# Layer 1 of a two-layer gated cross-attention kernel: the queries' rounding, the block transposition and the output's low part change places

## The reference, cut to what matters

```
q = rms_norm(latents @ Wq);  k = rms_norm(concat(context, latents) @ Wk);  v = concat(...) @ Wv
scores = einsum('bhgqd,bhkd->bhgqk', qg, k) / sqrt(128)
probs  = softmax(scores)
out    = einsum('bhgqk,bhkd->bhgqd', probs, v)
x      = x + tanh(g_xattn[1]) * (out @ Wo)
```

## Time and profile before

| | before |
|---|---|
| median of three runs | 1704.34 us |
| the profiled execution | 1706.54 us, its span 1704.7 us |
| PE busy | 1643.4 us (96%) |
| DVE busy | 1230.3 us (72%) |
| ACT busy | 1022.6 us (60%) |
| POOL busy | 589.8 us (35%) |
| first and last `nb` of layer 1's units | 958.4 and 1663.7 us |

### The profile page before, as it was taken

The page is one execution under the profiler, slowest core; times in us unless marked ns, Lnnn a source line. Parts: engine busy times, 40 slices in busy tenths (PEclk is TensorE's granted clock), DMA queues, the critical chain, the costliest instruction groups (busy, mean ns, idle before and its releaser), DMA issues.

```text
span 1704.7 us, 30549 instructions
## 1 busy us (share of the span) xinstructions
PE 1643.4 (96%) x9757; PEld 1436.2 (84%) x9757; DVE 1230.3 (72%) x2274; ACT 1022.6 (60%) x2511; POOL 589.8 (35%) x584
## 2 busy tenths in 40 slices
PE   9999999999999999999999799999999999999987
PEld 8899999999988888888888678888888888888875
DVE  6444437676787777877778677878787878777775
ACT  5344443345867677677766566666666666666652
POOL 3422223211334444444335333333333333333332
PEclk9999999999999999999999899999999999999999
DMA  6444444535233333333332243434343434343322
GB/s 231 171 166 148 148 171 157 191 133 182 72 106 102 120 98 111 113 95 126 98 106 82 72 136 122 148 119 146 118 159 123 145 123 148 123 148 111 115 93 97
DMA packets 126671, 220.43 MB, mean 129 GB/s; under 512 B 11664, under 2 KB 96016, under 8 KB 123024
## 3 DMA queue, kind: packets, MB, share of 16 engines
q1 hardware_dynamic: 126608, 219.63, 38.6%
HBM read 141.99 MB, written 77.59 MB: 129 GB/s over the span
## 4 chain that ended last, share of the span: by engine, by line
PE 58%; DVE 20%; ACT 9%; DMA 6%; issue 5%; SPq 1%; POOL 1%; DVEq 0%; ACTq 0%; POOLq 0%
PE bank L2134 20%; PE bank L2079 8%; PE bank L2080 8%; PE bank L2081 8%; PE bank L2311 6%; ACT p L1235 4%; DMA probabilities_transposed<-blocks_of_probabilities 2%; DMA blocks_of_probabilities<-probabilities_in_blocks 2%; DVE pt_lo L1957 2%; PE bank L2269 2%; PE bank L2347 2%; DVE probabilities_in_blocks L1966 2%; PE bank L2431 2%; DVE w_lo L1896 2%; DVE wl L1575 1%
## 5 line engine op out<-in xcount | busy, mean ns | idle before, releaser
L630 POOL TENSOR_TENSOR q_r<-q_ms,half 128x4 f32<-128x4 f32 x64 | 64.4, 1007 | 378.5 <-DVE q_ms L1922 378.5
L2079 PE MATMUL bank<-w_hi,xt_hi 128*128 (+2 forms) x512 | 173.4, 339 | 0.1
L2080 PE MATMUL bank<-w_lo,xt_hi 128*128 (+2 forms) x512 | 173.2, 338 | 0.0
L2081 PE MATMUL bank<-w_hi,xt_lo 128*128 (+2 forms) x512 | 172.0, 336 | 0.0
L711 POOL TENSOR_TENSOR pr<-pr,rn 128x512 f32<-128x512 f32 x64 | 67.5, 1055 | 291.4 <-DVE rn L1600 291.4
L1235 ACT ACTIVATE p<-bank,nb,q_r 128x256 f32<-128x256 f32 x256 | 141.4, 576 | 7.4 <-DVE nb L1943 7.4
L764 POOL TENSOR_TENSOR p<-p,rn 128x512 f32<-128x512 f32 x128 | 133.1, 1041 | 28.7 <-DVE rn L1948 25.2
L1244 ACT ACTIVATE pt_hi<-probabilities_transposed 128x1024 fp32r<-128x1024 f32 x64 | 68.0, 1063 | 94.6 <-DMA probabilities_transposed<-blocks_of_probabilities 94.6
L1075 ACT ACTIVATE pr<-sc,nmax 128x128 f32<-128x128 f32 x256 | 99.9, 391 | 40.0 <-DVE nmax L1585 39.6
L2079 PE MATMUL bank<-w_hi,ot_hi 128*128 (+1 forms) x256 | 107.3, 419 | 16.7 <-DVE ot_lo L1971 15.8
L2079 PE MATMUL bank<-w0o_hi,ot_hi 128*128 128x512 f32 x256 | 105.4, 412 | 5.0 <-DVE residual L1592 4.5
(11 more groups left out here) (292 smaller groups left out, 5574.6 us busy)
## 6 DMA issues: line engine op xcount, KB each, us to landing
blocks_of_probabilities<-probabilities_in_blocks SPq DMA_DIRECT2D x64, 512.0 KB, 2.7
probabilities_transposed<-blocks_of_probabilities SPq DMA_DIRECT2D x256, 128.0 KB, 2.8
stage<-w SPq DMA_DIRECT2D x35, 512.0 KB, 3.3
keys_of_layer<-kout SPq DMA_DIRECT2D x16, 1024.0 KB, 4.8
values_of_layer<-vout SPq DMA_DIRECT2D x16, 1024.0 KB, 5.2
kt<-keys_of_layer SPq DMA_DIRECT2D x64, 256.0 KB, 3.3
vs<-values_of_layer SPq DMA_DIRECT2D x64, 256.0 KB, 2.8
vraw<-wv SPq DMA_DIRECT2D x10, 1024.0 KB, 6.7
```

The lines of the kernel that those rows point to most:

```text
L630: pool.tensor_tensor(dst, src, exponent, ALU.pow).then_inc(done, 1)
L2079: nc.tensor.matmul(out_ap, l_hi, r_hi, start=(c == 0), stop=False)
L2080: nc.tensor.matmul(out_ap, l_hi, r_lo, start=False, stop=False)
L2081: op = nc.tensor.matmul(out_ap, l_lo, r_hi, start=False, stop=(c == n - 1))
```

## The change

On ACT, the roundings `qt_hi` and `kt_hi` of unit i+1 go ahead of the four exponentials of unit i. On DVE, `qt_lo` and `kt_lo` go ahead of the reciprocals; the two reciprocals are parted, with `v_low` between them; the block transposition of unit i goes ahead of `probabilities_lo` of i-1; `split_lo` goes from before the accumulation to after `probabilities_lo`; and `output1_lo` goes ahead of `maxima1`. No instruction is added or removed, and PE, POOL and SP keep their order. (Without `...` the diff also names the call of `inverse_sums1` after the loop, which is written as two.)

```
@@ ACT slot1
-                if not (first and j == 0):
-                    exponentials1(i, (j - 1) % 2)
                 act.wait_ge(qt1_ps, i + 1)
                 nc.scalar.activation(qt_hi[:, :], QTB[:, :], ACT.Copy).then_inc(qt1_hi_done, 1)
                 act.wait_ge(kt1_ps, i + 1)
                 nc.scalar.activation(kt_hi[:, :], KTB[:, 0:256], ACT.Copy, scale=kw[:, 0:1]).then_inc(kt1_hi_done, 1)
+                if not (first and j == 0):
+                    exponentials1(i, (j - 1) % 2)
@@ DVE
-            def inverse_sums1(count):
-                for half_p in (0, 2):
-                    dve.wait_ge(exp1_done, 2 * count - 1 + half_p // 2)
-                    nc.vector.reciprocal(rn1[:, half_p:half_p + 2], sum1[:, half_p:half_p + 2]).then_inc(recip1_done, 1)
+            def inverse_sums1(count, half_p):
+                dve.wait_ge(exp1_done, 2 * count - 1 + half_p // 2)
+                nc.vector.reciprocal(rn1[:, half_p:half_p + 2], sum1[:, half_p:half_p + 2]).then_inc(recip1_done, 1)
@@ DVE slot1
-                if lag1:
-                    inverse_sums1(i)
                 dve.wait_ge(qt1_hi_done, i + 1)
                 ...
+                if lag1:
+                    inverse_sums1(i, 0)
                 if ahead:
                     v_low(i + 2, (j + 1) % 4)
+                if lag1:
+                    inverse_sums1(i, 2)
+                if ahead:
                     k_scaled(i + 2, (j + 1) % 4)
+                if not (first and j < 3):
+                    accumulate1(i - 2, (j - 3) % B)
+                if lag1:
+                    probabilities_in_blocks(i)
+                if not (first and j < 2):
+                    probabilities_lo(i - 1, (j - 1) % 2)
                 if not last and 1 <= j < 6:
                     split_lo(t + 1, j - 1, (t + 1) % 2)
-                if not (first and j < 3):
-                    accumulate1(i - 2, (j - 3) % B)
-                if not (first and j < 2):
-                    probabilities_lo(i - 1, (j - 1) % 2)
-                if not (first and j < 1):
-                    probabilities_in_blocks(i)
...
+                if not (first and j < 2):
+                    output1_lo(i - 1)
                 maxima1(i + 1, j % 2)
...
-                if not (first and j < 2):
-                    output1_lo(i - 1)
```

More of the change, by code:

```diff
@@ L2036, in _ @@
             last_gate = tg[:, 3:4]
-            inverse_sums1(U)
+            inverse_sums1(U, 0)
+            inverse_sums1(U, 2)
             feed_forward(3, last_gate, 0)
```

## The result

The changed kernel takes 1763.87 us (median of 4 runs, 1760.46 to 1766.77), the kernel before 1704.34 (4 runs, 1704.03 to 1705.15): a ratio of 1.0348, interval 1.0324 to 1.0371. It is slower by 59.5 us where 11 were forecast, and lies outside the range of 1695 to 1737.

The account below looks back on a forecast made before the run. The prediction took the kernel as bound by PE, other engines holding it up at times. Slots behind a piece going from 11.15 to 11.91 us, others shorter, gave +11 us: 1715 us from 1704.34, range 1695 to 1737.

Parts of the forecast that it names:

- I take 0.9, since size and distance are those of the case: SP's queue: the probabilities' write behind a piece's load lands 0.9 us late, like the second of two 512 KB loads.
- the prediction's own loop: From one `pt_lo` to the next through SP's queue: 11.01 us plus the write's extra 0.9, so 11.91 a slot.
- The sum: Slots of groups 1 to 6 lengthen behind a piece, others shorten; groups 0 and 7 unchanged: together +11 us.
- The rivals' prices: Times of rival cases for slots with a piece, counted over 33 slots: 1686, 1736 and 1672 us.
- in line behind the whole piece: Rival, SP's queue: the write waits for the whole piece, some 1.5 us extra, +31 us, 1736 us; chance 0.20.
- The write isn't held up by the piece: Rival, SP's queue: the write lands 0 to 0.4 us late, 1686 us at zero; chance of a little-held-up write 0.22.
- The closed loop: SP and DVE: write waits for `split_lo`, that for `pt_lo`, that for the preceding round trip; 11.91 us a slot.
- the compute loop: PE, ACT and DVE from `pt_lo` through attention output and exponentials to `pt_lo`: 10.6 us where nothing else is late.
- Only the compute loop decides: Rival: SP is released early enough in all slots, so all 33 take 10.6 us instead of 11.91: 1672 us; chance 0.06.

Follow-up runs that it names:

- `split_lo` early: The changed kernel with the weight piece's low part (`split_lo`) back ahead of the accumulation on DVE: 1722.71 us, ratio 1.0109 to the kernel before.
- the first experiment: The changed kernel with SP issuing the probabilities' round trip ahead of the wait for the weight piece and its load: 1660.97 us, ratio 0.9747 to the kernel before.

## Why the prediction was wrong

**The step that failed** is "I take 0.9, since size and distance are those of the case". For c, the extra time of a write issued 0.40 us behind a piece, it used a pair of loads. In the changed kernel the 25 writes behind a piece in the loop take 4.75 to 5.10 us until their reads are issued, 4.97 in the median (5.01 in the turn above); less the 2.68 that it took alone, c is 2.29. With that the prediction's own loop is 11.01 + 2.29 = 13.30, and the four intervals between the pieces of a loop body are on average 13.35 to 13.43 us long, except the first body's 13.69.

This is most of the loss, but not all. The sum counted 28 intervals behind a piece, so c makes 28 x 1.39 = 39 of the 49 us between 1715 and 1763.87. (The rivals' prices count 33 of them, the sum 28: the two don't go together.) From the write of j = 0 in one head group to that in the next, groups 1 to 5 grew by 55.6 us where 12.4 were forecast, group 6 by 3.0 where it was to shrink by 1.2; group 0, which has five pieces too and was left out as unchanged, grew by 5.0, and group 7 shrank by 3.6.

**The upper bound failed as well.** The rival "in line behind the whole piece" gave c = 1.52, from a write 1.22 us behind a piece with an excess of 0.70, extended by the difference in distance. The excess by distance behind a load of 512 KB: 2.29 at 0.48 us (changed kernel), 0.70 at 1.22, 0.3 at 1.74 (`split_lo` early), nothing at 2.35 or more (the slots of before, write 2.7). The 0.70 was not chance: with `split_lo` early, two writes at 1.21 and 1.22 have 0.87 and 0.77. From 0.48 to 1.22 it falls by 1.59 in 0.74 us, twice as fast as in a queue in which a microsecond of distance saves a microsecond. The straight line was drawn through one point with an assumed slope. Its end had been called the end of the range, so the range missed too. The Trainium skill's fit for a transfer issued by GpSimd, 2.0 us plus bytes over 436 GB/s ("DMA: Bandwidth & Descriptors", section "Anatomy of one DMA — SWDGE (gpsimd) path"), had given an estimate of 0.8. The pair of loads and the pair of writes, which SP issues here, come near it (0.9 each), and a write behind a load does not.

**"The write isn't held up by the piece"** is out: in the loop's 25 pairs the load landed 4.0 to 4.3 us after its issue, and the write at the earliest 5.2 us after the load's issue.

**What was right.** The closed loop, and every other term of it: the load follows `w_lo` by 0.16 for 0.17, the write the load by 0.48 for 0.40, the reads take 4.27 for 4.30. Slots in which nothing is late are 10.49 us in the first experiment for a forecast of 10.6; but there PE is busy for 200.00 of the 200 us from 1100 on and shows no wait in layer 1, so it is PE's own work that sets them, and the compute loop is shown only to be no longer than that. PE's wait before the attention output rose above 1 us, and its wait for `ot_lo` went. The direction came from the closed loop.

**"Only the compute loop decides"** gave 1672 us on the condition that SP is released early enough. The condition did not hold in the changed kernel; where it was made to hold, the time was 1661.

**What was left out** is the clock. Windows of the changed kernel around one long wait, and the matmul behind that wait:

```profile
1220.49:1234.00 13.51, 10.56 (x60) 9.08 (x59) 8.77 (x21) 6.81 (x20) 4.12 (x5) 0.97 0.56 181
1234.00:1244.00 10.00, 10.00 (x51) 8.74 (x50) 6.67 (x17) 5.97 (x19) 3.46 (x4) 0.87 0.16 45
1244.00:1254.00 10.00, 10.00 (x59) 8.75 (x58) 7.65 (x19) 7.51 (x21) 3.76 (x4) 1.00 0.37 118
```

```profile
1232.84 0.50 PE L2082 MATMUL bank<-pt_hi,v_hi 128*128 128x512 f32 x1 [2.95 <-DVE pt_lo L1956]
```

PE waited 2.95 us, and in the 10 us from 1234 on the granted clock is 0.87, a mean of its two levels (1.2 and 2.4 GHz), with 51 matmuls done in place of 59. Its share of the loss is small: the stretches behind the last piece of a body are 46.10 us long (230.49 / 5) where the forecast's terms give 43.71; 1.39 of the difference is the fifth write's c above 0.9, and the 1.0 that remains makes 5 us in five bodies. How much of that is the clock isn't shown: in the third body nothing remains (44.91 us), at a granted clock of 0.95.

**What stays open** is why a write behind a load waits 1.4 us longer than a write behind a write or a load behind a load. The runs show that it goes with the load's bytes and with the order, that the load ahead is late too (4.2 us for 3.3), and that it is gone at 2.4 us of distance. What happens to the write's packets in between was not resolved.

## What to carry to other kernels

When an edit moves an instruction that a DMA queue waits for, follow the queue's next entries, and look for a transfer on a critical loop that lands behind one that nobody is waiting for: here swapping two neighbouring issues was worth 83 of 1764 us, and the round trip put ahead altogether turned the loss of 59 into a gain of 43. A price for two transfers in one queue belongs to their directions and their order; a pair of loads doesn't price a write behind a load, and where no row shows the pair at the distance in question, the range has to reach beyond a straight line. A change of several orders is judged as a whole: with the round trip first, one part undone cost 6 us (1666.62), 24 (1684.75) or 187 (1848.14 against 1660.97).

## What the runs showed of the hardware that was not expected

- In one queue, transfers of 512 KB: a write behind a load issued 0.4 to 0.5 us earlier lands in about 5.0 us instead of 2.7, and the load in 4.2 instead of 3.3; behind a write it lands in 3.6; ahead of the load in 2.9, with the load in 4.0. Behind a load of 128 KB it takes 3.3.
- DVE's scaling of 128x128 float32 keys that lie in SBUF took 0.83 us when it started 0.3 us into POOL's two multiplications, 0.27 when it started 0.9 us into them (first experiment), and 0.28 in its usual place. The low part of a weight piece took 1.84 us, starting 1.4 us into them (`split_lo` early), and 1.22 elsewhere.
